# Two layers of cross-attention and routed experts on one core: steps, set-up and turn in another order, and the residual rows kept on chip

## What is computed

```python
x = x + L0_xattn(layernorm(x), ctx)     # 8 heads of 8 channels, rotary positions, output projection
x = x + L0_ffn(layernorm(x))            # top 8 of 64 experts: silu(x Wg) * (x Wu), then Wd
x = x + L1_xattn(layernorm(x), ctx)     # 8 heads, no rotation, no output projection
x = x + L1_ffn(layernorm(x))            # top 8 of 64, and at most 128 rows of each block of 512 tokens' picks per expert
```

## Time and profile before

| | us |
|---|---|
| median of 3 runs | 2247.05 (2241.72 to 2247.66) |
| the profiled execution's own time | 2246.79 |
| its span in the trace | 2245.0 |
| PE busy | 1681.1 (75%) |
| DVE busy | 1462.2 (65%) |
| ACT busy | 1329.7 (59%) |
| POOL busy | 985.9 (44%) |

### The profile page before, as it was taken

The page is one execution under the profiler, slowest core; times in us unless marked ns, Lnnn a source line. Parts: engine busy times, 40 slices in busy tenths (PEclk is TensorE's granted clock), DMA queues, the critical chain, the costliest instruction groups (busy, mean ns, idle before and its releaser), DMA issues. The chain is left out here.

```text
span 2245.0 us, 45332 instructions
## 1 busy us (share of the span) xinstructions
PE 1681.1 (75%) x12724; PEld 1129.2 (50%) x12879; DVE 1462.2 (65%) x4525; ACT 1329.7 (59%) x3396; POOL 985.9 (44%) x1111
## 2 busy tenths in 40 slices
PE   1688888889882797999998177777777778756551
PEld 0355555555541686888987034444444444444431
DVE  3588888888863343555533378888889888853331
ACT  0377777777770454666665368777787878642110
POOL 1236666666666000000000665555556554128883
PEclk9799999999995898999999589999999999978996
DMA  4766767667647986666565676676667666338856
GB/s 150 206 179 180 185 180 186 185 182 190 178 129 218 311 275 204 184 189 186 183 192 176 171 190 175 171 170 172 169 171 173 169 168 164 93 114 200 186 103 109
DMA packets 420684, 399.24 MB, mean 178 GB/s; under 512 B 46171, under 2 KB 392667, under 8 KB 420443
## 3 DMA queue, kind: packets, MB, share of 16 engines
q1 hardware_dynamic: 345163, 264.16, 43.6%
q0 software_dynamic: 37904, 90.22, 16.3%
q10 hardware_dynamic: 37376, 41.96, 6.4%
HBM read 242.00 MB, written 178.42 MB: 187 GB/s over the span
## 5 line engine op out<-in xcount | busy, mean ns | idle before, releaser
L1009 DVE TENSOR_REDUCE mx<-psS 128x2 f32<-128x512 f32 x1024 | 691.1, 682 | 152.9 <-PE psS L1376 128.1
L818 ACT ACTIVATE prob<-psE 128x512 f32<-128x512 f32 x1024 | 598.2, 600 | 253.3 <-PE psE L1387 244.9
L702 POOL DMA_INDIRECT yg<-y_d,posb x256 | 265.0, 1035 | 764.8 <-DVE posb L1051 511.9
L1387 PE MATMUL psE<-q,k 128*128 128x256 bf16 x2048 | 396.6, 276 | 36.7 <-DMA q<-mlo 14.2
L1376 PE MATMUL psS<-k,q 128*128 128x512 bf16 x869 | 337.7, 391 | 60.2 <-DMA k<-k_stack_d 48.1
L1492 PE MATMUL psE<-wt,xgT 128*128 (+1 forms) x1536 | 327.6, 337 | 3.0 <-ACT xgT L910 2.6
L1328 DVE TENSOR_TENSOR hid<-sil,psE 128x96 f32<-128x96 f32 x384 | 97.4, 254 | 356.8 <-ACT sil L915 356.8
L690 POOL DMA_INDIRECT xs_d<-xr,posi x256 | 251.3, 982 | 105.9 <-ACT prob L818 66.3
L910 ACT COPY xgT<-psS 128x256 f32<-128x256 f32 x384 | 144.5, 376 | 228.8 <-PE psS L1486 209.3
L1403 PE MATMUL psO<-prob,v 128*32 128x256 f32 x4096 | 276.6, 388 | 0.8 <-ACT osb L799 0.8
L1387 PEld LDWEIGHTS psE<-q,k 128*128 128x128 bf16 x2048 | 189.9, 99 | 166.1 <-ACT prob L818 34.9
(11 more groups left out here) (212 smaller groups left out, 2630.5 us busy)
## 6 DMA issues: line engine op xcount, KB each, us to landing
xg<-xs_d SPq DMA_DIRECT2D x320, 128.0 KB, 2.5
y_d<-y_all SPq DMA_DIRECT2D x320, 128.0 KB, 2.1
q<-q_stack_d SPq DMA_DIRECT2D x128, 256.0 KB
k<-k_stack_d SPq DMA_DIRECT2D x128, 256.0 KB
wt<-in_gu ACTq DMA_DIRECT2D x128, 192.0 KB, 3.8
wt<-in_dn ACTq DMA_DIRECT2D x128, 96.0 KB, 4.4
q_stack_d<-parts SPq DMA_DIRECT2D x64, 192.0 KB
k_stack_d<-parts SPq DMA_DIRECT2D x64, 192.0 KB
```

Of the source, the lines that this page charges most:

```text
L702: g.indirect_dma_start(yg[:, k, :], None, y0_d[:, :], bass.IndirectOffsetOnAxis(posb[b][:, k:k + 1], 0)).then_inc(d_yg, 16)
L818: a.activation(prob[gr][:, u % 4, :], psE[ring][:, :], ACT.Exp, scale=SCALE).then_inc(s_exp, 1)
L1009: v_.tensor_reduce(mx[b][:, bg // 4, :].rearrange("p (h r) -> p h r", h=2)[:, :, (bg % 4) * 2 + tt], psS[(UNITS * (st.s0 - LAG["smax"]) + ...
L1387: ins = m_.matmul(psE[ring][:, i * T:(i + 1) * T], k2[b][:, bg, hh * T + i * P:hh * T + (i + 1) * P], q2[b][:, bg, :], start=True, stop=True)
```

## The change

It does the following:

- **Residual rows.** `xres`, `x2_d` and their loads and stores go. Layer 0 loads x straight into one of eight tiles `x2` (`KEEP = 8`), layer 1 sums into it, and `front`, `comb` and `back` all read it there.
- **Set-up.** The memsets of k go to POOL; sin and bias_c are loaded by ACT; x and ctx of pair 0 are loaded before the barrier; the pads and zero rows are written after it, in step 0, and waited for at the first `stack`.
- **Clears.** 64 clears of 128 rows, two per step from step 4, for the eight large ones; `odd_d` is zeroed in 33 DMAs, at tile 64 and each seventh after it. The first weights load in steps 9 to 14, not 0 to 5.
- **Turn.** Tiles of an expert end at its last row and begin in the zero rows ahead of its region; only expert 0 begins at its own start. One clear of an end stays. `clear_ends` becomes `clear_end`, on SP alone, and `tiles_table` works out the first rows in a new way.
- **Steps.** SP's order becomes: load, (layer 1's xn_d store), the parts, max rows 1, ctx, stack loads, clears, max rows 0, store. mT1 moves from unit 2 to 1, RK from 1 to 2, mT0 from 10 to 9, the rotation of k from 5 to 4, `nt` from 9 to 8, `place` and what follows it one unit later, hote and hotr of layer 1 from units 0 and 1 to 1 and 4. In layer 1 the gathers go at units 1 to 10 (`PACE`), all eight ahead of POOL's two splits.

The diff, cut to its core:

```diff
-CLEARS = 8
+CLEARS = E
+CLEAR_AT = 4
...
+AHEAD = 9
...
+ODD_EVERY = 7
 NB = 3
 
-PACE = (0, 2, 4, 6, 8, 10, 12, 14)
+KEEP = 8
+
+PACE = ((0, 2, 4, 6, 8, 10, 12, 14), (1, 2, 3, 5, 6, 7, 9, 10))
 
 COMB = 1
 SUM = 10
@@ -81,8 +88,8 @@
 
...
-    layer: [("RK", "place"), ("mT1", "attn"), ("V", "smax"), ("K", "front"), ("OT0", "back"), ("OT1", "back"),
-            ("Q", "front"), ("NT", "back"), ("XT", "route"), ("mT0", "smax"), last, ("LG", "route")]
+    layer: [("mT1", "attn"), ("RK", "place"), ("V", "smax"), ("K", "front"), ("OT0", "back"), ("OT1", "back"),
+            ("Q", "front"), ("NT", "back"), ("mT0", "smax"), ("XT", "route"), last, ("LG", "route")]
...
+        def clear_end(eng, engine):
+
 
             eng.wait_ge(s_guard, 1)
             eng.wait_ge(d_zero, 16 * CLEARS)
-            for first in range(half * FB, E, 2 * FB):
-                _, ends = nc.values_load_multi_w_load_instructions(
-                    guard[0:1, first:first + FB], engines=(engine,),
-                    min_val=0, max_val=DISPATCH - P, skip_runtime_bounds_check_because="the rows are clamped")
-                for end in ends:
-                    eng.dma_start(xs_d[bass.ds(end, P), :], xn_d[TOKENS:TOKENS + P, 0:T])\
-                       .then_inc(d_ends[group_of(first)], 16)
+            _, ends = nc.values_load_multi_w_load_instructions(
+                guard[0:1, 0:1], engines=(engine,), min_val=0, max_val=DISPATCH - P,
+                skip_runtime_bounds_check_because="the row is clamped")
+            eng.dma_start(xs_d[bass.ds(ends[0], P), :], xn_d[TOKENS:TOKENS + P, 0:T]).then_inc(d_small, 16)
 
         def sp_slot(st, first_row):
             sp = nc.sync
             if st.on("gather"):
                 b, job = st.buf("gather"), st.job("gather")
...
-                for g in range(len(ENDS)):
-                    if job == sum(ENDS[:g]):
-                        sp.wait_ge(d_ends[g], ends_before[g] + 16 * ENDS[g])
-                if job == ZERO_ODD:
-                    sp.dma_start(odd_d.rearrange("(n p) t -> n p t", p=P),
-                                 xn_d[TOKENS:TOKENS + P, 0:T].unsqueeze(0).broadcast_to((PAIRS + 1, P, T)))\
+                if job == 0:
+                    sp.wait_ge(d_small, 16 * 6)
+                if job >= ZERO_ODD and (job - ZERO_ODD) % ODD_EVERY == 0 and (job - ZERO_ODD) // ODD_EVERY <= PAIRS:
+                    sp.dma_start(odd_d[row((job - ZERO_ODD) // ODD_EVERY), :], xn_d[TOKENS:TOKENS + P, 0:T])\
                       .then_inc(d_zero, 16)
...
+            def load_x(st):
+
+                b, t = st.buf("load"), st.pair("load")
+                hold(sp, s_xn, last(st, "load", back=NB))
+                if st.L == 0:
+                    hold(sp, s_x1, last(st, "load", back=KEEP))
+                    sp.dma_start(x2[st.kept("load")][:, :], x[row(t), :]).then_inc(d_x[b], 16)
+                else:
+                    sp.dma_start(xin[b][:, :], x1_d[row(t), :]).then_inc(d_x[b], 16)
+
+            def load_ctx(st):
+
+                b, t = st.buf("comb"), st.pair("comb")
+                hold(sp, s_vp, last(st, "comb", back=NB))
+                sp.dma_start(ctx_t[b][:, :], ctx[row(t), :]).then_inc(d_ctx[b], 16)
+
+            load_x(Step(0, LAG["load"]))
+            load_ctx(Step(0, LAG["comb"]))
+            by_channel(sp, cos, tables[0])
+            barrier(sp, 1)
             zeros = xn_d[TOKENS:TOKENS + P, 0:T]
-            barrier(sp, 1)
+
...
+                first = L == 0 and st.s0 == 0
+                if st.on("load") and not first:
+                    load_x(st)
+                if first:
+                    set_up()
                 if st.on("post") and L == 1:
...
+                if st.on("attn"):
+                    b = st.buf("attn")
+                    for i, (part, made) in enumerate(((mhi[1], s_mhi[1]), (mlo[1], s_mlo[1]))):
+                        sp.wait_ge(made, st.n("attn"))
+                        sp.dma_start(q2[b][MAXROW + i:MAXROW + i + 65:64, 4:8, :].rearrange("p g t -> p (g t)"),
+                                     part[:, :]).then_inc(d_max[1][b], 16)
+                if st.on("comb") and (L == 1 or st.s0 > LAG["comb"]):
+                    load_ctx(st)
...
+                    if st.s0 == LAG["stack"]:
+                        if L == 0:
+                            sp.wait_ge(d_setup, 16 * (2 + 2 * NB))
+                        else:
+                            sp.wait_ge(s_clear, 2)
...
+                if L == 0 and 0 <= st.s0 - CLEAR_AT < PAIRS:
+                    for e in (2 * (st.s0 - CLEAR_AT), 2 * (st.s0 - CLEAR_AT) + 1):
+                        sp.dma_start(xs_d[bass.ds(e * STRIDE + LAST, P), :], zeros).then_inc(d_zero, 16)
...
-                if st.on("comb") and L == 1:
-                    b, t = st.buf("comb"), st.pair("comb")
-                    hold(sp, s_x2, st.n1("comb"))
-                    sp.dma_start(x2_d[row(t), :], x2[b][:, :]).then_inc(d_x2[b], 16)
...
+                for k in (4, 5) if L == 0 else (4, 5, 6, 7):
+                    moved(k, PACE[L][k])
...
+            by_channel(act, sin, tables[1])
+            by_channel(act, bias_c, wts["bias"])
...
-                    if u == 15 and st.s0 < EARLY // 2:
-                        for e in (2 * st.s0, 2 * st.s0 + 1):
+                    if u == 15 and 0 <= st.s0 - AHEAD < EARLY // 2:
+                        for e in (2 * (st.s0 - AHEAD), 2 * (st.s0 - AHEAD) + 1):
...
-                    if L == 1 and u == 2 and st.on("post"):
+                    if L == 1 and u == 3 and st.on("post"):
...
+                    if L == 0 and u == 8 and st.on("back"):
+                        act.wait_ge(s_ntp, st.n("back"))
+                        wait(act, s_wo, last(st, "back"))
+                        a.activation(nt[:, :], psM[item_bank(0, "NT")][:, 0:T], ACT.Identity,
+                                     bias=bias[:, 7:8]).then_inc(s_nt, 1)
...
-                    if u == 2 and st.on("attn"):
+                    if u == 1 and st.on("attn"):
...
-                    if u == 2 and st.on("place"):
+                        clear()
+                    if u == 3 and st.on("place"):
...
+                    if L == 1 and u == 8 and st.on("back"):
+                        b = st.buf("back")
+                        dve.wait_ge(s_ntp, st.n("back"))
+                        wait(dve, d_x1[b], lastbuf(st, "back"))
+                        v_.scalar_tensor_tensor(x1[b][:, :], psM[item_bank(1, "NT")][:, 0:T], bias[:, 8:9],
+                                                x2[st.kept("back")][:, :], ALU.add, ALU.add).then_inc(s_x1, 1)
...
-                    if u == 0 and st.on("post") and L == 1:
+                    if u == 1 and st.on("post") and L == 1:
...
-                    if L == 0 and u == 5 and st.on("front"):
+                    if L == 0 and u == 4 and st.on("front"):
+                        if st.s0 == LAG["front"]:
...
-                    if u == 1 and st.on("post") and L == 1:
+                    if u == 4 and st.on("post") and L == 1:
...
+                link(v_.scalar_tensor_tensor(cnt[:, 6, :], cnt[:, 2, :], float(P), cnt[:, 0, :], ALU.mult, ALU.subtract))
+                link(v_.memset(cnt[:, 6, 0:1], 0.0))
+                link(v_.memset(cnt[:, 7, E - 1:E], 0.0))
+                link(v_.tensor_tensor(cnt[:, 6, :], cnt[:, 6, :], base0[:, :], ALU.subtract))
...
+                link(v_.tensor_tensor(cnt[:, 4, :], cnt[:, 3, :], cnt[:, 2, :], ALU.subtract))
+                link(v_.scalar_tensor_tensor(cnt[:, 5, :], cnt[:, 4, :], float(P), cnt[:, 6, :], ALU.mult, ALU.add))
+                link(v_.tensor_tensor(cnt[:, 7, 0:E - 1], cnt[:, 5, 0:E - 1], cnt[:, 5, 1:E], ALU.subtract))
...
+                    link(v_.tensor_tensor(cmpm[:, c, :], cmp_[:, c, :], cnt[:, 7, :], ALU.mult))
...
-                link(v_.tensor_reduce(owner[:, 1, :], cmpm[:, :, :], AX.X, ALU.max))
-                link(v_.tensor_tensor(owner[:, 2, :], slotk[:, :], owner[:, 1, :], ALU.subtract))
-                link(v_.tensor_scalar(owner[:, 3, :], owner[:, 2, :], float(P), None, ALU.mult))
-                link(v_.scalar_tensor_tensor(owner[:, 3, :], owner[:, 0, :], float(STRIDE), owner[:, 3, :],
-                                             ALU.mult, ALU.add))
+                link(v_.tensor_reduce(owner[:, 1, :], cmpm[:, :, :], AX.X, ALU.add))
...
+                    if u == 1 and st.on("attn"):
+                        product("mT1", "attn", [(s_max, st.n("attn", UNITS))],
+                                [(mx[st.buf("attn")][:, 1, :], None)], s_mT[1])
+                    if u == 2 and st.on("place"):
+                        b = st.buf("place")
+                        product("RK", "place", [(s_mask, st.n("place"))],
+                                [(tri0[:, :], mask[b][:, :]), (ones[:, :], mask[b][:, :])], s_rkp, E)
...
+                    if u == 9 and st.on("smax"):
+                        product("mT0", "smax", [(s_max, st.n("smax", UNITS, 8))],
```

(1 more changed line is left out.)

175 lines of the change are left out of this document (57 added, 118 removed).

## The result

The kernel after the change took 2181.81 us (median of 4 runs, 2177.69 to 2186.34), the kernel before 2244.39 beside it (2239.94 to 2247.66): a ratio of 0.972, with a 95% interval of 0.969 to 0.975. So it is faster, by 62 us, where I had forecast 130, and outside my range of 2060 to 2175. The profiled execution took 2185.0, its span 2183.3.

A forecast was written before the change was run, and what follows sets the result against it. It took the attention steps to be bound by a ring of three engines waiting in turn, with three plain holes outside them. Terms 30 + 27 + 14 + 18 + 38 + 3 = 130 took 2247 to 2117 us, range 2060 to 2175.

The forecast's parts named there:

- Start: Start to first products: earlier barrier and first product on xn, plus clears leaving steps 1 to 8; 30 us, 25 to 35.
- Layer 0: Attention steps of layer 0: earlier k load, rotation and mT0 save 0.9 per step; 27 us over 30 steps, 8 to 45.
- Turn: From layer 0's attention to its experts: fewer end clears, so PE starts at 726.7 instead of 740.71; 14 us, 9 to 17.
- the load land in 3: At the turn: the first tile load was to land in 3 us, without 8 MB ahead, and PE then start.
- Burst: Layer 0's expert tiles: splitting the 4.2 MB zeroing of odd_d into 33 removes a slow window; 18 us, low end 14.
- filling of layer 1: Start of layer 1: gathers 6 and 7 ahead of POOL's splits shorten ACT's wait for gathered rows; 3 us, 0 to 7.
- Layer 1: Attention steps of layer 1: 1.4 less in each of 23 steps, 0.7 in eight emptier ones; 38 us, 12 to 64.
- the walk: One layer 1 step, durations added along ACT and PE: unit 8's reduction 1.2 earlier, plus 0.2 for late k.
- the steps keep their length: Rival: the ring of waits closes again elsewhere, only holes outside the steps go; 65 us, 2182 us, chance 0.13.
- Slower by mT1: Rival: mT1 asks for the last reduction a unit earlier, PE stops each step; 85 us lost, 2267 us, chance 0.03.
- The split clears: Rival: the split clears crowd the queue, burst gives 10 and layer 0 steps 12; 2140 us, chance 0.10.
- The signs: V copies 17.9 apart in layer 0, 20.5 in layer 1; turn wait near 20; wrong if layer 1 DVE idle stays 2.8.

The follow-up runs named there:

- e12: Kernel before with only products mT1 and RK exchanged, in units and banks, place and total at unit 3: 2251.43 us, ratio 0.991.
- f4: Kernel after with SP's old order, max rows of the second half ahead of the stores of the parts: 2190.70 us, ratio 0.977.
- f3: e6 with PE's wait for the second group of expert weights moved from slot 8 to slot 16: 2109.30 us, ratio 0.940.
- e1: Kernel after with DVE's four additions of gathered rows in layer 1 starting at unit 9 instead of 10: 2155.15 us, ratio 0.961.
- e6: Kernel after with DVE's additions one unit earlier, POOL's first subtraction held until they are done, ACT's second copy one unit later: 2109.50 us, ratio 0.940.
- e3: Kernel before with only POOL's new order and pacing of layer 1, all eight gathers ahead of its two subtractions: 2284.87 us, ratio 1.018.
- e5: Kernel after with only the order of RK and mT1 in the PSUM bank table put back, units kept: 2224.28 us, ratio 0.991.
- e9: e6 with PE's wait for the second group of expert weights at slot 16, on a chip with slower layer 0: 2180.44 us, ratio 0.960.
- e10: Kernel before with only the residual rows kept on chip in eight buffers: 2269.52 us, ratio 0.999.

## Why the prediction was wrong

**Start: right** (33 against 30, inside 25 to 35, to the second copy of V). The barrier and the first product on xn stand within 1 us of where I put them, and the second k, whose wait I named, lands in time. The 25 of the table's first row is the barrier's part alone.

**Layer 0: right in sign, wrong in the parts, 36 against 27 for thirty steps, inside 8 to 45.** I named k (0.9), the rotation (0.6) and nt (0.6) and left mT1's exchange as a danger. Measured, the exchange alone is a gain of 0.6 per step (e12) and SP's order, from which I took the gain on k, 0.28 (f4); the 0.3 that is left of the 1.20 has the rotation and mT0 in it, not tried alone. Two steps failed. I read mT1's move only as a unit nearer to the last reduction, a possible loss. And the 14.0 that I quoted for k is the row of PE's weight loads, which overlap its matmuls; in the same window PE itself stood less than half of that for k, 0.45 per step:

```profile
PE psS L1376 <- DMA k<-k_stack_d: 6.7, 6, 1.6
```

**Turn: 6 against 14.** The first half, from the last scatter to the first tile load, was to fall by 7.3 and fell by 5.5. The second, from that load to PE, was to fall by 6.7 and fell by 0.2. It rests on the sentence "the load land in 3". The row that I quoted, says "<-DMA wt<-in_dn": PE waited for weights, those that the kernel loads only behind the barrier, and not for the tile. f3 shows that, and also that taking the wait away would not have paid.

**Burst and filling of layer 1: right** (18.6 against 18, 2.1 against 3).

**Layer 1: the step that failed the prediction.** I added the durations of the kernel before along ACT and PE and moved POOL's gathers ahead, "the splits end later", with no price for where they end. The durations of DVE's two additions were not constants: they held only because neither subtraction of POOL ran beside them, with 0.02 us to spare on one side. The step went from 21.92 to 23.55 where I had it fall by 1.4. The collision itself is worth 1.7 (e1 to e6) to 2.0 per step (e3); I had it at nothing, without a reason.

Without the collision the time came out near the walk: e6's step is 1.31 shorter than the kernel before's, and its 31 steps take 42 less (665.4 to 623.4; I had 38). That is weaker than it looks as a proof of the walk, since e6 also has the additions a unit earlier, worth 1.21 in e1 and not in my sum. That e6 took 2109.5 where I had forecast 2117 is in part luck: its layer 0 gave 41 in the table's count and its turn 7.

**The rivals.** The time of the first (2182, the steps keep their length) came out within a microsecond, and it is wrong all the same: layer 0 got 44 shorter and layer 1 33 longer. "Slower by mT1" is refuted: alone in the kernel before, the exchange makes it 20 faster (e12). The split clears did not crowd the queue: the burst gave 18.6, and the window of tiles with them in it runs at full clock, 14.20 for 92 matmuls. I had no rival in which an instruction of DVE gets longer. The signs that I had named do tell it: DVE's idle time in layer 1 is 2.6 per step, hardly below the 2.8 at which I called the prediction wrong, V copies are 23.55 apart (I said 20.5), and PE's wait at the turn is 28.02 (I said near 20).

## What to carry over

Before an instruction of POOL is moved in time, list DVE's instructions that read two operands from SBUF (and casts) near its new place: each one that it met here ended only when POOL's instruction had, 0.9 to 1.1 us late for a 0.4 us addition and 1.2 for a 0.15 us cast, and the engines behind it wait in turn. If they can't be kept apart by position, a semaphore that makes POOL wait can be cheaper than the meeting (from e1 to e6, with ACT's copy a unit later, 1.55 of waiting bought 1.73 per step). And when products are reordered in a ring of shared PSUM banks, follow for each which reader of the bank it now waits for: in e5 two names in the old order cost 42 us. Last, when one edit is taken back to price it, ask what else has moved with it: e5's wait for `total` is in neither the kernel before nor the kernel after.

## What the runs showed that I had not expected

It goes against POOL too: a gather that is issued as DVE's 1.2 us addition of two SBUF operands begins takes 2.08 instead of 0.95 (at 1539.47 in the kernel after, across DVE's 1539.53 to 1540.74). Between 1300 and 1800 the 21 gathers that lie beside this addition take 2.09 at the median, the other 148 0.95. And in the set-up of the kernel after a cast of 128 columns took 1.91 while POOL cleared k until 8.5; in the kernel before, with no POOL instruction beside it, it took 0.22. That these are the same port is not tried by itself.

```profile
3.17 5.35 POOL L674 MEMSET k<- 128x2048 f32 x3 [0.15 <-issue]
6.69 1.91 DVE L993 CAST iota_r<-iota_i 128x128 bf16<-128x128 int32 x1
```

Chips differ by more than some of these edits: on one of the four that the experiments fell on, e9's layer 0 took 19.07 per step against 17.53 for the same code, and its layer 1 21.76 against 20.61 in e6. The kernels built on the kernel before lost little there in layer 0 (18.89 in e10), but took 105 from the last copy of V to the first tile, against 91. In e9 the durations of the instructions are the same; ACT stands some 0.55 at a time, 28 times in fifteen steps, where the trace names nobody that it waits for. What holds it is open.
